# A hand-ordered one-core pipeline of a scan block and two expert networks: other offsets, and a denser table for the first and last two batches

## The reference

```python
x = x + 0.5 * ffn(layernorm(x))     # 8 experts of width 344, all computed, two of them weighted per token
x = x + mamba(layernorm(x))         # 4 layers, then @ Wout + bout
x = x + 0.5 * ffn(layernorm(x))     # the same expert weights again

# one of the 4 layers of mamba
xp, z = split(rmsnorm(h) @ Win)                   # 256 channels each
xc = silu(causal_conv4(xp) + b)
dt, Bm, Cm = split(xc @ Wx)
delta = softplus(dt @ Wdt + bdt)
state[t] = exp(delta[t] * A) * state[t-1] + delta[t] * xc[t] * Bm[t]      # 256 channels x 16 states
y[t] = sum(state[t] * Cm[t]) + xc[t] * Dp
h = h + (y * silu(z)) @ Wblk
```

## Time and profile before

| | |
|---|---|
| median of 3 timed runs | 4988.75 us (4970.44 to 4993.5) |
| the profiled execution | 4979.66 us, its span 4977.9 us |
| POOL busy | 4291.9 us, 86% |
| DVE busy | 4264.4 us, 86% |
| PE busy | 4094.9 us, 82% |
| ACT busy | 3473.1 us, 70% |
| mean granted clock of TensorE | 0.903 |

### The profile page before, as it was taken

How to read it: one execution, slowest core, us unless ns; L and a number is a source line. 1 busy time by engine, 2 the same in 40 slices (tenths; PEclk the granted TensorE clock), 3 DMA queues, 4 the chain that set the end, 5 groups by cost and what they waited for, 6 DMA issues and landing times.

```text
span 4977.9 us, 50492 instructions
## 1 busy us (share of the span) xinstructions
PE 4094.9 (82%) x11584; PEld 1329.8 (27%) x11584; DVE 4264.4 (86%) x5503; ACT 3473.1 (70%) x5275; POOL 4291.9 (86%) x2281
## 2 busy tenths in 40 slices
PE   6867676898888888888888888888888888585878
PEld 2212121232222223222232223232222222121223
DVE  2656897999999999999999999999999998895753
ACT  3555675777777777777777777777777777564553
POOL 0556999999999999999999999999999999996750
PEclk9877786999999999999999999999999998696879
DMA  1232334443344334443344433443334433442220
GB/s 58 54 78 64 86 83 105 102 96 78 91 105 105 85 80 98 104 104 83 81 102 104 100 75 86 105 105 88 82 95 104 103 77 81 103 105 52 53 52 5
DMA packets 136627, 425.15 MB, mean 85 GB/s; under 512 B 15886, under 2 KB 35279, under 8 KB 135952
## 3 DMA queue, kind: packets, MB, share of 16 engines
q1 hardware_dynamic: 136335, 421.92, 34.9%
HBM read 145.04 MB, written 8.39 MB: 31 GB/s over the span
## 4 chain that ended last, share of the span: by engine, by line
POOL 29%; PE 25%; issue 19%; DVE 15%; ACT 6%; DMA 3%; SPq 2%; DVEq 0%; POOLq 0%; ACTq 0%
POOL work L783 16%; POOL work L773 10%; DVE work L593 7%; PE b_ps L334 4%; PE y_ps L306 4%; PE a_ps L328 3%; PE b_ps L322 3%; POOL dd_src L792 2%; PE s_ps L394 2%; DMA dd_sb<-dd_src 2%; DVE s_ps L649 2%; SPq L264 2%; PE s_ps L381 2%; PE a_ps L315 1%; DVE sg_sb L683 1%
## 5 line engine op out<-in xcount | busy, mean ns | idle before, releaser
L783 POOL TENSOR_TENSOR work<-dd_sb,bc_sb 128x1024 f32<-128x1024 f32 x1024 | 2406.0, 2359 | 179.1 <-DMA dd_sb<-dd_src 108.9
L593 DVE TENSOR_TENSOR_SCAN work<-dA_ps,work 128x512 f32<-128x512 f32 x2048 | 2400.7, 1207 | 84.0 <-ACT dA_ps L441 58.6
L441 ACT ACTIVATE dA_ps<-dd_sb,a_sb 128x512 f32<-128x512 f32 x2048 | 1356.5, 681 | 597.5 <-DVE work L593 504.5
L773 POOL TENSOR_TENSOR work<-work,bc_sb 128x1024 f32<-128x1024 f32 x704 | 1660.2, 2359 | 13.0 <-DVE work L593 13.0
L306 PE MATMUL y_ps<-work,sel_sum 128*32 128x512 f32 x4096 | 625.6, 686 | 231.7 <-POOL work L773 189.7
L334 PE MATMUL b_ps<-sg_sb,wd_sb 128*128 128x512 f32 (+1 forms) x1536 | 748.9, 617 | 62.7 <-DVE sg_sb L683 62.6
L322 PE MATMUL b_ps<-xT_sb,wg_sb 128*128 128x512 f32 (+1 forms) x1024 | 610.8, 680 | 127.7 <-DVE acc_sb L668 81.5
L328 PE MATMUL a_ps<-xs_sb,wu_sb 128*128 128x512 f32 (+1 forms) x1024 | 563.4, 633 | 9.6 <-DVE sg_sb L683 9.5
L683 DVE TENSOR_TENSOR sg_sb<-sg_sb,a_ps 128x512 f32<-128x512 f32 (+1 forms) x512 | 344.1, 672 | 223.9 <-PE a_ps L328 222.7
L334 PEld LDWEIGHTS b_ps<-sg_sb,wd_sb 128*128 128x128 f32 (+1 forms) x1536 | 291.9, 196 | 473.3 <-issue 307.1
L473 ACT ACTIVATE sg_sb<-b_ps 128x512 f32<-128x512 f32 (+1 forms) x512 | 303.6, 593 | 156.9 <-PE b_ps L322 147.9
(11 more groups left out here) (99 smaller groups left out, 4275.9 us busy)
## 6 DMA issues: line engine op xcount, KB each, us to landing
dd_sb<-dd_src SPq DMA_DIRECT2D x512, 512.0 KB, 8.6
bc_sb<-bc_rows SPq DMA_DIRECT2D x256, 512.0 KB, 4.9
xr_sb<-in_L_attn_x SPq DMA_DIRECT2D x16, 256.0 KB, 6.1
bc_rows<-dbc_sb SPq DMA_DIRECT2D x128, 32.0 KB, 1.6
out<-xr_sb SPq DMA_DIRECT2D x16, 256.0 KB, 6.9
wg_sb<-in_L_ffn_Wg SPq DMA_DIRECT2D x1, 1376.0 KB
wu_sb<-in_L_ffn_Wu SPq DMA_DIRECT2D x1, 1376.0 KB
wd_sb<-in_L_ffn_Wd SPq DMA_DIRECT2D x2, 512.0 KB
```

The costliest lines, as they stand in the source:

```text
L441: act.activation(dA_ps[:, g % NDA, :], dd_sb[:, b, c, 0, :], ACT.Exp, scale=a_sb[:, l, b, j, c:c + 1]).then_inc(dA_ready, 1)
L593: dve.tensor_tensor_scan(tile, dA_ps[:, g % NDA, :], tile, 0.0, ALU.mult, ALU.add).then_inc(scanned, 1)
L773: pool.tensor_tensor(work[:, g % RING], work[:, g % RING], bc_sb[:, j, 0, :].unsqueeze(1).broadcast_to([128, 2, T]), ALU.mult).then_inc(po ...
L783: pool.tensor_tensor(work[:, g % RING], dd_sb[:, b, 2 * (i % 2):2 * (i % 2) + 2, 1, :], bc_sb[:, j, 1, :].unsqueeze(1).broadcast_to([128, ...
```

## The change

Three things change; no instruction, shape or buffer is added or dropped.

1. **The table of phases.** Batches 2 to 13 have layer l in window 4n - 3 + 3l. The first and last two batches have windows of their own, with their layers as close as two windows. Windows 1 to 63 hold a phase each, and one phase is in window -1; window 0 is the only empty one between them.
2. **The starts of the units.** FFN1 of batch n starts in window 4n - 8 at tick 22, with batches 0, 1 and 2 in ticks -4W - 96, -2W - 96 and W (each + 22); FFN2 in window 4n + 10, with batch 13 in window 60, batch 14 at 63W + 96 and batch 15 at 65W + 96 (each + 22).
3. **The offsets.** The post of a phase stands at ticks 14 to 25 of the window behind it instead of 19 and 88 to 108. Its prep stands at ticks 20 to 143 of the window ahead instead of -11 to 123. The offsets within a scan, an expert, a start and an end change too: for instance POOL's four small steps of a start (`gap`, `den`, `comb`) all stand on tick -13, where they stood on -34, -32 and -24.

```diff
-CORE = {"exp": -12, "scan": -1, "dbu": -14, "dve_prod": 8, "pool_prod": 11, "c": -3, "sum": 28, "y0": 89, "y1": 19}
-PREP = {"sq": -11, "ms": 8, "rms": 7, "xn": 16, "xp0": 15, "conv0": 16, "xp1": 26, "conv1": 24, "silu_xc": 30, "z0": 38,
-        "zc0": 30, "z1": 40, "zc1": 34, "silu_z": 62, "wx": 46, "dbc": 45, "rows": 25, "dt0": 53, "sp0": 49, "delta0": 62,
-        "du0": 72, "dt1": 77, "sp1": 71, "delta1": 81, "du1": 106, "dd0": 90, "dd1": 123, "bc": 79}
-POST = {"wblk": 88, "h": 96, "attn": 107, "x2": 108}
-FFN_AT = {"gb": 3, "xs": 5, "g0": 10, "g1": 10, "g2": 10, "burst": 8, "u0": 18, "u1": 18, "u2": 25, "hh0": 19, "hh1": 20,
-          "hh2": 27, "down": 32, "acc": 37}
-START = {"load": -130, "bn": -81, "nb": -63, "xtok": -48, "xt": -39, "xT": -46, "lg": -35, "lg_sb": -36, "mx": -35,
-         "mi": -35, "gap": -34, "we": -38, "eq": -24, "den": -32, "inv": -28, "comb": -24, "ct": -14, "gates": -18}
-END = {"yt": 15, "xo": 10, "bn": 42, "nb": 82, "xtok": 90, "ht": 105, "h": 104, "store": 75}
+CORE = {"exp": -10, "scan": -1, "dbu": -10, "dve_prod": 14, "pool_prod": 9, "c": 5, "sum": 33, "y0": 89, "y1": 14}
+PREP = {"sq": 20, "ms": 32, "rms": 29, "xn": 38, "xp0": 44, "conv0": 41, "xp1": 52, "conv1": 49, "silu_xc": 56, "z0": 60,
+        "zc0": 56, "z1": 67, "zc1": 62, "silu_z": 88, "wx": 75, "dbc": 67, "rows": 33, "dt0": 80, "sp0": 75, "delta0": 81,
+        "du0": 85, "dt1": 107, "sp1": 98, "delta1": 107, "du1": 143, "dd0": 82, "dd1": 120, "bc": 67}
+POST = {"wblk": 17, "h": 17, "attn": 22, "x2": 25}
+FFN_AT = {"gb": 0, "xs": -1, "g0": 1, "g1": 4, "g2": 6, "burst": 2, "u0": 8, "u1": 18, "u2": 22, "hh0": 13, "hh1": 18,
+          "hh2": 24, "down": 27, "acc": 29}
+START = {"load": -130, "bn": -53, "nb": -56, "xtok": -48, "xt": -21, "xT": -26, "lg": -11, "lg_sb": -14, "mx": -14,
+         "mi": -10, "gap": -13, "we": -9, "eq": -5, "den": -13, "inv": -6, "comb": -13, "ct": -2, "gates": -8}
+END = {"yt": 3, "xo": 0, "bn": 10, "nb": 11, "xtok": 25, "ht": 91, "h": 88, "store": 113}
...
-    table = {}
-    for n in range(B):
-        for l in range(NL):
-            table[4 * n + 3 * l] = (n, l)
+    table = {4 * n - 3 + 3 * l: (n, l) for n in range(2, B - 2) for l in range(NL)}
+    end = 4 * B
+    for n, windows in ((0, (-1, 2, 4, 7)), (1, (1, 3, 6, 10)), (B - 2, (end - 11, end - 8, end - 4, end - 2)),
+                       (B - 1, (end - 7, end - 5, end - 3, end - 1))):
+        for l, w in enumerate(windows):
+            table[w] = (n, l)
...
-FFN = sorted([(W * (4 * n - 5) + 22, 1, n) for n in range(B)] + [(W * (4 * n + 13) + 22, 2, n) for n in range(B)])
+FFN1_AT = {0: -4 * W - 96, 1: -2 * W - 96, 2: W}
+FFN2_AT = {B - 3: W * (4 * B - 4), B - 2: W * (4 * B - 1) + 96, B - 1: W * (4 * B + 1) + 96}
+FFN = sorted([(FFN1_AT.get(n, W * (4 * n - 8)) + 22, 1, n) for n in range(B)] +
+             [(FFN2_AT.get(n, W * (4 * n + 10)) + 22, 2, n) for n in range(B)])
...
-                if t == -W - 4:
+                if t == -2 * W:
```

More of the change, by code:

```diff
@@ L61 @@
 NORM_OF = {(what, f): m for m, (_, what, f) in enumerate(NORMS)}
-FIRST, LAST = FFN[0][0] + START["load"], FFN[-1][0] + E * PERIOD + END["h"] + 1
+FIRST, LAST = FFN[0][0] + START["load"], FFN[-1][0] + E * PERIOD + max(END["h"], END["store"]) + 1
 XSLOTS, HSLOTS = 6, 4
```

## The result

The changed kernel takes 4907.78 us in the median (4905.01 to 4910.41) against 4982.48 us (4970.44 to 4993.5) for the kernel before on the same chip: a ratio of 0.9851, 95% interval 0.9824 to 0.9877. That is 1.5% faster, where 4862 us and 2.5% were forecast; it lies inside the range. The profiled execution has a span of 4903.2 us.

What follows compares the result with a forecast made beforehand. POOL was taken to bound the body, with DVE right behind. The span was 193 + (69.5 + 50) + 62 x 69.5 + 64 + 169 = 4854.5 us, giving 4862 predicted; own range 4825 to 4918, 8-in-10 range 4775 to 4970.

Steps and rivals of the forecast that it cites:

- the gap: One gap left between windows -1 and 1, taken as 50 us where four gaps together cost 199.6 us before.
- the head: Stretch to the first `dbu`, forecast at 193 us, a loss of 17 us, with unit 1 following unit 0 at once.
- rival C: Close pairs wait: preps of layers two windows apart wait for h, up to 8 us each, 4910 us; chance 0.10.
- D: Rival: empty windows close but head and tail take it back at their worst, pace unchanged, 4898 us; chance 0.05.
- The 64 us of the last scan: Term for the stretch of the last scan, between the body's windows and the tail, kept at 64.0 us as before.
- -2.1 + 1.2 + 0.8 = -0.1: Body's pace: waits gained, start's cost, and a quarter of DVE's 2.9 us; 69.5 us a window taken, from 69.6.
- both waits of POOL [...] could go: POOL's waits for `dd_sb` and the sum gain 2 to 3 us of room and could go: -2.1 us a window.
- (a): POOL's steps of a start on one tick, nothing between while DVE and ACT answer: 2.4 us a unit, 1.2 a window.
- (b): h at once behind `y1`: DVE stands for 0.7 us, or 2.1 with the hand-overs and PE late.
- (c): Delta has 25 ticks from ACT's burst instead of 32, so DVE may stand for 1.5 us.
- it costs nothing now: Shorter distances on POOL, `dbu` to scan 13 to 9 ticks, scan to product 8 to 6, counted only in the upper end.
- The body 66 us faster: Eq short again gives DVE 1.1 us a window; sum 66 us lower if DVE alone set the pace; left out.

## Why the prediction was right, and where it was not

The direction, the gap, the head and the turn between the last units hold to 1 or 2 us. **Gaps and ends:** one gap of 118.2 - 70.2 = 48 us (50 forecast), and between windows 1 and 63 none: the windows between the close pairs took 65 to 72 us (1 to 2 took 65.5, 2 to 3 70.0) and the others 67 to 76, so rival C didn't occur. Nor did D; the tables alone gained 112 of the 117 us forecast. The forecast itself has a slip of 3 us: 4856 and the 9 us to the median are 4865, not 4862.

**The tail and the last scan.** The 64 us of the last scan were read where the window ahead was empty, and I carried them over without asking what now stands beside it. POOL is busy for 68.9 of the 73.3 us, before for 61.3 of 64. The 7.6 us more are two products of the scan of window 62, the second half of `du` and the norm steps of unit 30's start; before, none of them fell into this stretch. The other 1.7 us are idle: POOL waits 3.55 us for the last scan, before 2.26. The first accumulation of unit 30 came 10 us behind the last scan instead of 15, as `y1` came 5.0 us behind it, before 8.8. The prediction put the 8.8 down to POOL's products, and that was wrong: POOL's last product ends 2.4 us behind the last scan after and 2.5 before. The rest is TensorE's queue, where the sum began 1.4 us later, before 3.5, and DVE's, which before stood at an expert's product in front of `y1`. Net 6 us.

**The body's pace** is the step that failed, though the time lies inside the range: the term "-2.1 + 1.2 + 0.8 = -0.1". By its parts, from the waits of 800 to 4200 us:

- "both waits of POOL [...] could go": that for `dd_sb` went from 0.97 to 0.40 us a window. That for the sum rose from 1.06 to 2.22. I counted POOL's ticks between a product and the `dbu` that needs its tile (15 to 21) and not how late the product's own scan can be. -2.1 should have been +0.6. Even without the table loads the two waits together did not fall: 1.15 + 0.69 us a window with the old offsets, 0.40 + 1.49 with the new.
- (a), 1.2 us a window: POOL waits 22.7 us at L829 in 24 starts, 0.5 a window. Too high, and taking the new start back costs 5057.2 - 4907.8 = 149 us.
- (b), 0.7 to 2.1 us: DVE waits for h 22.3 us in 48 windows, 0.46 each, below the low end.
- (c), 1.5 us: delta is not among DVE's seven largest waits, the last of which is 0.7 us in all. It cost next to nothing.
- Not in the sum at all: ACT's burst. I listed the shorter distances from `dbu` to scan and from scan to product as "it costs nothing now", and left out what stands between ACT's exponentials and DVE's scans. The exponential's own lead fell from 11 ticks to 9, but that isn't it by itself: three scans are left at the begin of every burst in both kernels. What shrank is DVE's other work that covers the rest of the burst, from 3.5 to 2.4 us. It is 187.3 us of DVE's time in 48.4 windows, 3.9 a window against 0.6 before.

That the pace came out within 0.7 us is partly luck: (a), (b) and (c) were priced too high and the gain of 2.1 us did not come. Without the loads the new offsets are worth -0.1 us a window, the number of the sum, but from other parts than the sum has.

DVE lost 3.3 us a window at the exponentials, but POOL stands idle for 1.0 more, and the pace lost 0.6. DVE got part of it back: its wait of 1.5 us a window for the experts' products (L683 before) is gone, though one of 0.9 for TensorE ahead of their gated inputs (L684 after) has come, and eq is short again. Eq after, 64 of them, summed over the program (line, operation, count, total us, mean ns, idle before):

```profile
L736 DVE TENSOR_TENSOR eq_sb<-iota_e,mf_sb 128x32 f32<-128x32 f32 x64 | 8.4, 172 | 0.0
```

and before:

```profile
L728 DVE TENSOR_TENSOR eq_sb<-iota_e,mf_sb 128x32 f32<-128x32 f32 x64 | 65.6, 1063 | 0.0
```

POOL now waits for DVE at this point instead of multiplying beside it: a `dbu` or a product of POOL ran during 58 of the 64 before and during none after. So 0.9 us each came back, 0.9 a window where I had 1.1. The Trainium skill (SBUF — State Buffer, "SBUF: two separate sides") has such a pair of operations exclude each other for a whole instruction; the trace agrees. The body 66 us faster did not come, as DVE alone doesn't set the pace.

**Shown and not shown.** That the offsets cost about 37 us, and that their cost in the body's pace is gone when the table loads are, is shown. That exponentials behind a burst are late, and ahead of which scans, is shown by the timelines. That it is DVE's smaller share of other work that uncovers the burst is read from the timelines, not tested by a run. Which single offset would give the 0.6 us back is open: `exp` back at -12 was not tried, and each of the others put back alone (sum, DVE's products, start, and with the old tables the post) made it slower.

## What to carry to other kernels

In an order written by hand, look for the longest block that can get in between a producer's items, and lay beside it what the consumer still has to do when the block begins, in time and not in ticks: here 5.2 us of ACT and an exponential against three scans of 3.6 us and DVE's other work among them, 3.5 us before and 2.4 after. A wait on a ring tile can be only where a stall arrives; one tile more shows it in a run, and if another wait takes its place the cause is upstream. Offsets that were found together could not be taken back one by one here, but tables and offsets can be told apart with one run.

## What the runs showed of the hardware

**Table loads on ACT.** In the place shown above a load is 1.28 us and the next exponential begins 1.29 us after the load did (2445.84 to 2447.13). The Trainium skill (ScalarE: Activation LUTs, "What ACT_TABLE_LOAD costs") gives about 2.66 us for a switch, a load of 1283 ns and a drain of about 1380. The load agrees. The drain doesn't show in this trace, and the measurement decides: the next activation stands right behind the load, and a burst of 5.2 us less two loads (2.6) and three SiLUs of 0.6 leaves 0.8 us, not two drains. What the loads cost was not ACT's time (ACT fell from 71% to 58% busy without them), but what was queued behind.

**TensorE's clock at small products.** Granted clock and busy times around the eight products with Wout and bout after (columns as in the earlier trace rows):

```profile
2432.50:2436.00 3.50, 3.50 (x9) 1.08 (x7) 2.77 (x4) 1.24 (x2) 3.50 (x3) 1.00 0.00 0
2436.00:2439.50 3.50, 3.50 (x17) 2.53 (x16) 3.50 (x5) 1.98 (x2) 3.50 (x2) 0.89 0.66 71
2439.50:2443.50 4.00, 4.00 (x7) 1.63 (x6) 3.61 (x4) 0.60 (x1) 4.00 (x3) 0.50 0.96 197
```

TensorE is busy throughout. Behind the last of 16 matmuls of 128 columns the granted clock is 0.50, 1.2 GHz, and two matmuls of 512 columns take 2.08 us, where they take about 1.1 us at full clock. From 800 to 4200 us these small products come 13 times, and 12 times the clock falls to 0.50 while they run; why, no run here takes apart. ACT waits in this burst for the products behind them with the SiLU table loaded, which is most of what makes it 9.5 us long: DVE's wait ahead of scan 9 is 4.6 us in the mean of these windows and 1.3 in the others. With the small products moved away DVE's longest wait fell from 5.1 to 3.1 us.
